# Two attentions with 16-wide heads: where TensorE issues the four quarters of values times probabilities

## The reference, cut to what matters

```python
scores = jnp.einsum('bhqd,bhkd->bhqk', query, key_h) * scale
scores = jnp.where(mask == 0, jnp.float32(-1000000000.0), scores)  # layer 0 only
attn = jax.nn.softmax(scores, axis=-1)
x = jnp.einsum('bhqk,bhkd->bhqd', attn, value)
```

## Time and profile before

| | |
|---|---|
| median of three runs | 3304.3 us |
| the profiled execution | 3303.58 us, span 3301.4 us |
| TensorE busy | 2793.6 us, 85% |
| VectorE busy | 1921.3 us, 58% |
| ScalarE busy | 1731.5 us, 52% |
| GpSimd busy | 849.6 us, 26% |
| attention of layer 0, units | about 94 to 393 us of the span |
| attention of layer 2, units | about 1601 to 1850 us of the span |

### The profile page before, as it was taken

How to read it: one execution, slowest core, us unless ns; L and a number is a source line. 1 busy time by engine, 2 the same in 40 slices (tenths; PEclk the granted TensorE clock), 3 DMA queues, 4 the chain that set the end, 5 groups by cost and what they waited for, 6 DMA issues and landing times. The chain is left out here.

```text
span 3301.4 us, 47876 instructions
## 1 busy us (share of the span) xinstructions
PE 2793.6 (85%) x14900; PEld 1573.7 (48%) x14900; DVE 1921.3 (58%) x4757; ACT 1731.5 (52%) x2884; POOL 849.6 (26%) x957
## 2 busy tenths in 40 slices
PE   7899879779999996657799789999668888888877
PEld 3233349734545453324222359997324444444453
DVE  6777641265565655006788511114589898999963
ACT  3566421156555653002577423332479898898853
POOL 4100020110000000003200030003467777777740
PEclk8899989989999999788899899999879898999998
DMA  5111156410000001891222339994410000100101
GB/s 168 46 54 48 58 192 227 165 37 0 1 1 1 1 1 79 357 395 62 82 59 59 114 133 351 343 346 163 149 34 20 20 25 10 26 19 10 26 29 47
DMA packets 161775, 326.54 MB, mean 99 GB/s; under 512 B 29408, under 2 KB 128480, under 8 KB 138208
## 3 DMA queue, kind: packets, MB, share of 16 engines
q1 hardware_dynamic: 152128, 304.78, 26.6%
q0 software_dynamic: 4608, 12.59, 1.2%
q10 hardware_dynamic: 4896, 7.35, 0.7%
HBM read 275.22 MB, written 49.28 MB: 98 GB/s over the span
## 5 line engine op out<-in xcount | busy, mean ns | idle before, releaser
L2870 POOL TENSOR_TENSOR L3x_fade<-L3x_behind,L3x_apart 128x1024 f32<-128x1024 f32 x128 | 280.0, 2187 | 155.9 <-DVE L3x_mx L3007 94.0
L2989 DVE TENSOR_TENSOR_SCAN L3x_behind<-L3x_first_exp,L3x_beside_scan 128x513 f32<-128x513 f32 x256 | 309.7, 1210 | 0.0
L1319 ACT ACTIVATE L1x_probs<-L1x_scores,L1x_neg_max 128x512 f32<-128x512 f32 x256 | 173.7, 684 | 218.5 <-DVE L1x_neg_max L1371 218.5
L1371 DVE TENSOR_REDUCE L1x_neg_max<-L1x_scores 128x2 f32<-128x1024 f32 x128 | 156.6, 1224 | 143.9 <-PE L1x_scores L1219 143.9
L2795 PE MATMUL L3x_probs_tp<-identity,L3x_fade 128*128 128x128 f32 x1024 | 169.3, 291 | 64.5 <-POOL L3x_neg_max_parts L2879 64.4
L1652 ACT ACTIVATE L2f_hiddenT<-L2f_hidden_ps,L2f_b1s 128x128 f32<-128x128 f32 x320 | 100.2, 364 | 208.3 <-PE L2f_hidden_ps L1587 208.3
L795 DVE CUSTOM_DVE_ANT_0 L0x_masked_scores<-L0x_s,L0x_mask_q 128x512 f32<-128x512 f32 x256 | 167.1, 685 | 61.3 <-issue 55.2
L2795 PEld LDWEIGHTS L3x_probs_tp<-identity,L3x_fade 128*128 128x128 f32 x1024 | 132.5, 150 | 141.2 <-POOL L3x_neg_max_parts L2879 80.8
L2907 ACT ACTIVATE L3x_first_exp<-L3x_scores,L3x_nm 128x512 f32<-128x512 f32 x256 | 181.7, 710 | 30.2 <-DVE L3x_nm L2981 27.7
L2981 DVE TENSOR_REDUCE L3x_nm<-L3x_scores 128x1 f32<-128x512 f32 x256 | 173.5, 678 | 34.0 <-PE L3x_scores L2775 33.9
L2935 ACT ACTIVATE L3x_probs_T<-L3x_probs_tp 128x512 f32<-128x512 f32 x256 | 159.2, 622 | 63.9 <-PE L3x_probs_tp L2798 63.9
(11 more groups left out here) (537 smaller groups left out, 6323.3 us busy)
## 6 DMA issues: line engine op xcount, KB each, us to landing
L2f_w1s<-in_L_w SPq DMA_DIRECT2D x40, 1024.0 KB, 7.5
L2f_w2s<-in_L_w SPq DMA_DIRECT2D x40, 1024.0 KB, 6.3
L1f_w1s<-in_L_w SPq DMA_DIRECT2D x32, 1024.0 KB, 16.0
L1f_w2s<-in_L_w SPq DMA_DIRECT2D x32, 1024.0 KB, 10.6
L0f_w1s<-in_L_w SPq DMA_DIRECT2D x16, 1024.0 KB, 6.0
L0f_w2s<-in_L_w SPq DMA_DIRECT2D x16, 1024.0 KB, 5.2
L0x_q_stack<-L0x_q_parts SPq DMA_DIRECT2D x96, 64.0 KB, 2.6
L0x_k_stack<-L0x_k_parts SPq DMA_DIRECT2D x96, 64.0 KB, 2.7
```

Source lines behind the costliest of these rows:

```text
L1319: nc.scalar.activation(p[:, n % 3, h, :], s[:, n % 2, h, :], ACT.Exp, bias=nmax[:, n % 4, h:h + 1], accum_out=den[:, n % 4, h:h + 1]).then ...
L2870: nc.gpsimd.tensor_tensor(fz[:, f:f + 2, :], bs[:, fb:fb + 2, 0:S], w, ALU.mult).then_inc(y_done, 1)
L2989: nc.vector.tensor_tensor_scan(bs[:, f, :], ex[:, t, :], beside[:, 0:1].to_broadcast([P, S + 1]), 0.0, ALU.add, ALU.bypass).then_inc(f_don ...
```

## The change

The quarters 0, 1 and 2 of `weigh` move from the end of the units r = 0, 1 and 2 to the middle of the units r = 1, 2 and 3: behind tiles 0 and 1 of `scores` and ahead of `turn_max`. Quarter 3 stays at the end of r = 3. So r = 0 has no quarter, r = 1 and 2 have one in the middle, r = 3 has one in the middle and one at the end. No instruction is added or taken away, and the other engines' programs stay.

```diff
                     shifted(u, i, 0)
                     if last > 2:
                         scores(u + 2, (i + 2) % 8, [0, 1])
+                    if r and not first:
+                        weigh(g + (-1), q, r - 1)
                     if r == 0 and not (isinstance(u, int) and u < 8):
                         turn_o(g + (-2), (q + 1) % 2)
                     if last > 1:
...
                     shifted(u, i, 1)
                     if last > 2:
                         scores(u + 2, (i + 2) % 8, [2, 3])
-                    if not first:
-                        weigh(g + (-1), q, r)
+                    if r == 3 and not first:
+                        weigh(g + (-1), q, 3)
```

## The result

Twenty executions of each kernel, in turns on the same chip: before 3303.39 us, changed 3313.45 us, ratio 1.0033 with a 95% interval of 1.0023 to 1.0044. The change costs 10 us; 3321 was forecast. The profiled execution of the changed kernel took 3309.55 us, its span is 3307.3 us. The numbers in brackets behind a ratio are such an interval in all that follows.

The account below looks back on a forecast made before the run. TensorE was taken to set the pace, with at most 26.1 us of idle ahead of quarters removable; longer unit cycles added 6.0 us (layer 0) and 11.4 (layer 2), 17.4 on 3303.6, giving 3321, range 3302 to 3332.

Parts of the forecast that it names:

- The likeliest case of the prediction: Both layers: moved quarters delay the maxima of tiles 2 and 3 and the next scores; 3321 us, chance 0.72.
- The wait of quarter 0 moves, it does not go: Layer 0, r = 1: tiles 0 and 1 wait for maxima instead of quarter 0 waiting; 4.31 us, +0.06.
- The new cycle: Tile 1, quarter, `turn_max`, second `shifted`, tile 2, maxima, next tile 1: layer 0 4.31 us against 4.13, layer 2 3.84 against 3.52.
- quarter to the next instruction 1.00: TensorE, quarter followed by `turn_max`: taken as 1.00 us, as before `shifted`; upper bound 1.09, shown by no row.
- the 0.09 between `scores` and `turn_max`: TensorE: `scores` to `turn_max` costs 0.09 us more than to `shifted`; used for the upper bound 1.09 behind a quarter.
- 0.42: Layer 0: forecast loss per full group, +0.42 us, from +0.06 in r = 1 and +0.18 each in r = 2 and 3.
- 0.83: Layer 2: forecast loss per full group, +0.83 us, from -0.27 (r = 0), +0.46 (r = 1), +0.32 each (r = 2, 3).
- the 17.4: Whole kernel: forecast loss of 17.4 us, 6.0 in layer 0 plus 11.4 in layer 2.
- r = 0 in layer 2, -0.27: Layer 2, r = 0: tile 3 of r = 3 no longer waits, so 4.33 us instead of 4.60.
- Rival 1: Quarter 0's wait in both layers goes and nothing replaces it: 26.1 us less, 3277.5 us; chance 0.06.
- Rival 2: The stall only moves; r = 2 and 3 stay bound by TensorE: 3302, up to 3306 us; chance 0.12.
- Rival 3: TensorE's clock falls to the lower level in one unit of ten: 30 us more, 3351 us; chance 0.05.

Follow-up runs that it names:

- Short maxima: Layer 2 maxima read 256 of 512 columns: in the kernel before 3283.76 us, ratio 0.993; in the changed kernel 3291.68 us, ratio 0.9949.

## Why the prediction was right, and where its sum was off

The likeliest case of the prediction happened, in direction, place and mechanism, and the measured time lies within the range. The loss was 10 us in place of 17, or 0.33%; I had given the largest chance, 0.52, to a loss of more than 0.5%, and it missed by the size of one term.

- *The wait of quarter 0 moves, it does not go.* Right. L722 lost its waits and L686 took them, and the run with quarter 0 alone moved shows this trade at zero in the whole, within 5 us either way. For r = 1 in layer 0 I forecast 4.31 us from last maximum to last maximum; it is 229.87 - 225.65 = 4.22, less than the 4.25 before.
- *The new cycle sets r = 1 to 3.* Right. Short maxima turn the changed order from 0.54 us slower to 0.22 us faster a group of layer 2.
- *Its terms.* Layer 0, from the rows after: 0.31 + 0.90 + 0.32 + 0.88, then 0.43 + 1.31 + 0.06 to the next tile 1, 4.21 us, against 4.31 forecast. The mis-sized term is "quarter to the next instruction 1.00". The prediction named it as shown by no row and bounded it from 1.00 to 1.09; it measured 0.90, outside. The other terms came as forecast to 0.01 us. In layer 2 the unit took 3.75 us against 3.84, the same 0.09 less. I had taken the 0.09 between `scores` and `turn_max` as a price of `turn_max`; behind a quarter, whose matmuls are narrow like those of `turn_max`, it is absent. That it is the price of a change of shape fits the rows and is not isolated. Three places a group at 0.1 us are 0.3 us: 0.42 - 0.30 = 0.12 and 0.83 - 0.30 = 0.53 a group, measured 0.15 and 0.54. Over 14 groups and two layers this term alone is 8 us of the 17.4.
- *r = 0 in layer 2, -0.27.* Right: 4.33 us, the number forecast.
- *Rival 1* (the wait goes, 3277) fell: the idle in view was slack of VectorE's order, not a price.
- *Rival 2* (r = 2 and 3 stay bound by TensorE) fell, by little in layer 0: +0.09 a unit.
- *Rival 3* (the clock) did not happen: from 113 to 393 and from 1613 to 1850 us the granted clock is 1.00, before and after. The run with `normalise` last shows it at waits of 1.3 and of 2.0 to 2.2 us.

The Trainium skill, TensorEngine Tiling (Array Packing), section Key Properties, says that changing the tiling mode drains the engine, while tiles of one mode run in parallel. This case fits both. Two matmuls of `scores` are followed by `shifted`, of their own shape, after 0.44 us (232.35 to 232.79 above) and by `turn_max` after 0.53; a quarter is followed by `shifted` after 1.00 and by `turn_max` after 0.90; and in one run a quarter starts 0.02 us behind `turn_max`. The page gives no price for the change. With the 0.09 of the rows as the price, and `turn_max` counted to the same mode as the quarter, the term would have been 0.91; I had not weighed that.

## What to carry to other kernels

A wait that the profile shows in front of an instruction is worth what the next wait behind it leaves. Before moving work into a gap, follow the buffers that go round between two engines and count how much of the producer's work stands between handing over a buffer and wanting it back: work taken from there stops hiding the consumer, and work put on the other side of the loop is paid in full. When two instructions get new neighbours on TensorE, price them by a pair of the same two shapes.

## What the runs showed of the hardware

- Small matmuls that write different groups of 32 output partitions run at the same time even when they belong to different steps and types: `turn_max` (bf16, partitions 96 and 97) starts at 233.68 us and the quarter (f32, 32 partitions a head) at 233.70, ahead of the other three transpositions, which stand before it in the program.
- In the run with `normalise` last TensorE waited once a group, 2.0 to 2.2 us in layer 0 and 1.3 us in layer 2, and ran at 1.2 GHz behind that in ten and in five of twelve groups. In the other runs the longest waits were 1.15 us (layer 0, ahead of quarter 0 in the order of before), and the granted clock is 1.00 from 150 to 350 and from 1650 to 1800 us.
- VectorE stands idle 0.57 us between reciprocal and a multiplication whose address comes from a loop register, and 0.43 us when the values are computed ahead, with the multiplication then 0.79 in place of 0.65 us in layer 0; in unrolled code it is 0.04 us.
